# A transformer layer on one core: 52 unread products in two places, a lead-in four steps earlier, and stores issued past two barriers

## What is computed

```python
def layer(x, W_attn, b_attn, W_proj, b_proj, fast_b, w_fc, w_proj, u, v, gate):
    x = x + attention(layernorm(x))          # 16 heads of 16, causal, float32 softmax, then @ W_proj + b_proj
    h = layernorm(x)
    a = bitlinear(h, w_fc) + gate * (h @ v.T @ fast_b.T @ u.T)     # 256 -> 1024
    r = maximum(a, 0.0)
    return x + bitlinear(r * r, w_proj)      # 1024 -> 256
def bitlinear(x, w):   # rows of w become -s, 0 or s with s = mean |w| of the row
    s = clip(mean(abs(w), axis=1), 1e-5)
    return x @ (s * clip(round(w / s), -1, 1)).T
```

## Time and profile before

| | us |
|---|---|
| median of 3 runs | 2120.4 |
| lowest and highest | 2115.23 and 2132.78 |
| the profiled execution, its own time | 2129.81 |
| its span in the trace | 2128.1 |
| busy in the span: PE, DVE, ACT, POOL | 2032.3, 1850.8, 1487.4, 474.8 |
| mean granted clock of TensorE | 0.967 of full |

### The profile page before, as it was taken

One profiled execution on the slowest core, in us unless ns is written; L12 is line 12 of the kernel. 1 busy time (PEld: TensorE's weight loads), 2 busy tenths in 40 slices (PEclk: granted clock), 3 DMA queues, 4 the chain that ended last, 5 costly groups with the idle time before them and its releaser, 6 DMA issues. The chain is left out here.

```text
span 2128.1 us, 46470 instructions
## 1 busy us (share of the span) xinstructions
PE 2032.3 (96%) x18173; PEld 1123.1 (53%) x18173; DVE 1850.8 (87%) x3143; ACT 1487.4 (70%) x2787; POOL 474.8 (22%) x637
## 2 busy tenths in 40 slices
PE   6987899999999999999999999999999969999998
PEld 5875344444444444444444444444444438888887
DVE  7987889999999999999999999999999438998996
ACT  2331378888888888888888888888888535555554
POOL 0000011011110111111011110111111127776774
PEclk9997599999999999999999999999999779999999
DMA  5995121221222212122121211212122122333220
GB/s 192 325 317 215 29 54 47 53 57 38 75 52 60 55 40 65 48 70 47 53 60 34 82 51 54 57 37 71 50 63 62 36 65 80 101 89 90 80 80 30
DMA packets 163003, 168.29 MB, mean 79 GB/s; under 512 B 74704, under 2 KB 102880, under 8 KB 162784
## 3 DMA queue, kind: packets, MB, share of 16 engines
q1 hardware_dynamic: 154112, 157.72, 25.4%
q10 hardware_dynamic: 8672, 7.60, 1.3%
HBM read 95.77 MB, written 67.63 MB: 77 GB/s over the span
## 5 line engine op out<-in xcount | busy, mean ns | idle before, releaser
L984 ACT ACTIVATE probs<-ps_s 128x512 f32<-128x512 f32 x2176 | 1179.3, 596 | 257.8 <-PE ps_s L1177 231.8
L1010 DVE TENSOR_REDUCE maxes<-ps_m 128x2 f32<-128x1024 f32 (+1 forms) x960 | 1141.9, 1220 | 110.5 <-PE ps_m L1140 88.4
L1198 PE MATMUL ps_acc<-probs,vs 128*32 128x256 f32 (+1 forms) x8696 | 703.9, 396 | 11.9 <-ACT acc_sb L962 11.9
L1177 PE MATMUL ps_s<-qs,ks 50*128 50x512 f32 (+3 forms) x2560 | 577.8, 450 | 1.0 <-ACT probs L984 0.9
L1140 PE MATMUL ps_m<-ks,qs 48*128 48x512 f32 (+3 forms) x2560 | 504.4, 392 | 18.7 <-DVE maxes L1010 9.5
L1177 PEld LDWEIGHTS ps_s<-qs,ks 50*128 50x128 f32 x2560 | 255.9, 186 | 414.0 <-ACT probs L984 381.1
L1198 PEld LDWEIGHTS ps_acc<-probs,vs 128*32 128x32 f32 x8696 | 173.7, 108 | 295.1 <-issue 194.7
L918 POOL TENSOR_SCALAR_AFFINE_SELECT probs<-probs 128x512 f32<-128x512 f32 x256 | 160.0, 640 | 744.1 <-ACT probs L984 740.5
L1140 PEld LDWEIGHTS ps_m<-ks,qs 48*128 48x128 f32 x2560 | 265.1, 192 | 94.5 <-DVE maxes L1010 70.7
L1017 DVE CUSTOM_DVE_ANT_0 sums_masked<-ps_m,mask 128x384 f32<-128x384 f32 (+1 forms) x512 | 186.6, 421 | 20.2 <-PE ps_m L1140 4.1
L1382 POOL TENSOR_TENSOR hid<-square,hid 128x512 fp32r<-128x512 f32 x128 | 175.3, 1378 | 107.3 <-DVE square L1393 91.9
(11 more groups left out here) (129 smaller groups left out, 1764.5 us busy)
## 6 DMA issues: line engine op xcount, KB each, us to landing
qs<-q_scr SPq DMA_DIRECT2D x384, 64.0 KB, 2.7
...
```

Source lines behind the costliest of these rows:

```text
L984: act.activation(probs[:, s % RING, x], ps_s[:, k % BANKS], ACT.Exp).then_inc(ring_taken, 1)
L1010: last = dve.tensor_reduce(maxes[c % 2][:, :, pairs, tt, i], banks, AX.X, ALU.max)
L1177: last = pe.matmul(ps_s[:, k % BANKS, at:at + width], ks[u][rows, j // TT, p, j % TT * P:(j % TT + 1) * P], qs[u][rows, c, p, q0:q0 + widt ...
L1198: last = pe.matmul(ps_acc[h * VW:(h + 1) * VW, q0:q0 + width], vs[u][:, j, h], probs[:, s % RING, h % banks_of(s), at:at + width], start=( ...
```

## The change

The new function `fill` issues products of 128 x 128 weights by 512 columns of `w_o` into a bank of PSUM that nobody reads before it is written anew. They wait for nothing and signal nothing. Three of them follow each of the last ten items of the opening (30 in all), two stand at each place for values of the first three steps of unit 0 (10), and two follow steps 17, 18, 19, 32, 33 and 34 of the last unit (12).

The places of the last unit move: turning u from step 17 to 16, its product from 22 to 20, w1 from 25 to 21, w2 from 29 to 25, the scales from 33 to 29, the projection from 34 to 31, and with them the loads and copies of chunk 0 (o from step 19 to 20, x from 22 to 24). DVE takes the factor (`take_low_factor`) before the second ternary weight. DVE's part of the projection, residual and variance is at step 31 and no longer behind the last step. The load and scaling of chunk 1's attention result go into the last unit (SP at step 32, POOL after its last step). ACT takes the root ahead of the last copy of the accumulator. At the start of feed-forward ACT copies `xn_t` ahead of chunk 1's o.

SP's stores of chunk 15 go to the start of block 2, and those of the last accumulator and reciprocal to the start of block 3, the reciprocal itself too (DVE). In block 1 the twelve small DMAs go from ACT to SP, ahead of SP's first store; PE's transposes of chunk 1 go behind chunk 0's products of q and k; and DVE's scaling of the weights no longer waits for the load of `w_o`.

```diff
-LOADS_AT, TERNARY_AT, O_AT, X_AT = 5, 16, 19, 22
-LOW_AT, G_AT, W1_AT, W2_AT, S_AT, PROJECT_AT = 17, 22, 25, 29, 33, 34
-SCALE_AT, BIAS_AT, O_HIGH_AT = 26, 30, 33
+LOADS_AT, TERNARY_AT, O_AT, X_AT, O1_AT = 5, 16, 20, 24, 32
+LOW_AT, G_AT, W1_AT, W2_AT, S_AT, PROJECT_AT = 16, 20, 21, 25, 29, 31
+SCALE_AT, BIAS_AT, O_HIGH_AT = 25, 29, 29
+
+
+FILLED_ITEMS, FILLED_STEPS = 10, (17, 18, 19, 32, 33, 34)
...
+def fill(pe, w_o, bank, count):
+
+    for _ in range(count):
+        pe.matmul(bank, w_o[:, 0, 0, 0:P], w_o[:, 0].rearrange("p k d -> p (k d)"), start=True, stop=True, skip_group_check=True)
...
+def store_acc(sp, scr, lead, n, c):
+
+    sp.wait_ge(lead.acc_copied, NCH * n + c + 1)
+    acc_sb, sums = lead.acc_sb[c % 2], lead.sums[c % 2]
+    for h in range(GH):
+        sp.dma_start(sums[h * VW:(h + 1) * VW, :],
+                     acc_sb[h * VW + HD:h * VW + HD + 1, :].rearrange("o (x e) -> o x e", x=VW)).then_inc(lead.sums_in[c % 2], 16)
+    dst = scr["o"].rearrange("b g r (c s) -> b g c r s", s=CH)[bass.ts(n // GROUPS, 1), bass.ts(n % GROUPS, 1), c]
+    sp.dma_start(dst.rearrange("o i r s -> (o i r) s"), acc_sb[:]).then_inc(lead.acc_stored[c % 2], 16)
+
+
...
+def store_chunk(sp, scr, sh, n):
+
+    u = n % 2
+    for m in range(4):
+        sp.wait_ge(sh.l_done, 4 * n + m + 1)
+        dst = (scr["q"] if m < KD else scr["k"]).rearrange("b a (f d) (c s) -> b f c d a s", f=KD, s=CH)
+        dst = dst[bass.ts(n // NCH, 1), m % KD, bass.ts(n % NCH, 1)].rearrange("o i d a s -> (o i d) a s")
+        sp.dma_start(dst, sh.parts[u][:, m].bitcast(F32)).then_inc(sh.parts_stored[u], 16)
+    sp.wait_ge(sh.v_copied, 2 * n + 2)
+    dst = scr["v"].rearrange("b p (c t) d -> b c p t d", c=NCH)[n // NCH, n % NCH]
+    sp.dma_start(dst, sh.v_out[u]).then_inc(sh.v_stored[u], 16)
...
+            sp.dma_start(w_o_in[:], io["W_proj"].rearrange("(k p) n -> p k n", p=P)).then_inc(w_o_loaded, 16)
+
+            sp.wait_ge(masked, 3)
+            for r in range(2):
+                for half in range(2):
+                    for dst, src in ((sh.ident_half, keep["ident_h"]), (sh.mask_half, keep["mask_h"])):
+                        sp.dma_start(dst[ROW * r:ROW * (r + 1), half], src[ROW * half:ROW * (half + 1), :]).then_inc(sh.fixed_in, 16)
+            sp.wait_ge(sh.ones_set, 1)
+            load_ones(sp, sh, sh.ks)
...
+                if left > 0:
+                    store_chunk(sp, scr, sh, n)
...
-            dve.wait_ge(w_in, 16 * 2)
+            dve.wait_ge(w_qkv_loaded, 16)
...
-            act.wait_ge(masked, 3)
-            for r in range(2):
-                for half in range(2):
-                    for dst, src in ((sh.ident_half, keep["ident_h"]), (sh.mask_half, keep["mask_h"])):
-                        act.dma_start(dst[ROW * r:ROW * (r + 1), half], src[ROW * half:ROW * (half + 1), :]).then_inc(sh.fixed_in, 16)
-            act.wait_ge(sh.ones_set, 1)
-            load_ones(act, sh, sh.ks)
...
-                if left >= 1:
+                if left >= 1 and n > 0:
...
+                if n == 0:
+                    transposes(1, 1)
...
+            store_chunk(sp, scr, sh, BATCH * NCH - 1)
...
-                if last:
-                    store_acc(n, NCH - 1)
-                    store_recip(n, NCH - 1)
+                    if last and s == O1_AT:
+                        sp.wait_ge(late.w2_ready, KH // 2)
+                        load_o(sp, scr, lead.o_in[1], lead.r_in[1], lead.o_loaded[1], 1)
...
+                if last:
+                    scale_o(pool, lead.o_in[1], lead.r_in[1], lead.o_loaded[1], lead.o_scaled, 1)
...
                 if last:
+                    lead.norm.take_root(act, 0)
                     copy_acc(n, NCH - 1)
-                    lead.norm.take_root(act, 0)
...
+                        take_low_factor()
...
+                    if last and s == PROJECT_AT:
+                        copy_low(dve, lead.o_t, lead.o_in[0], lead.o_copied, lead.o_split, 0)
+                        for i in range(2):
+                            residual(dve, lead, lead.x, lead.x1, 0, i)
+                        lead.norm.variance(dve, 0)
                 if last:
-                    copy_low(dve, lead.o_t, lead.o_in, lead.o_copied, lead.o_split, 0)
-                    for i in range(2):
-                        residual(dve, lead, lead.x, lead.x1, 0, i)
-                    lead.norm.variance(dve, 0)
                     lead.norm.normalise(dve, lead.x1, lead.xn, 0).then_inc(lead.xn_ready, 1)
-                    invert(n, NCH - 1)
...
+                    if x[1] >= LEAD - FILLED_ITEMS:
+                        fill(pe, keep["w_o"], ps_acc[:], 3)
...
+                        elif what == "values":
+                            fill(pe, keep["w_o"], ps_acc[:], 2)
+                    if last and s in FILLED_STEPS:
+                        fill(pe, keep["w_o"], ps_m[:, 3], 2)
...
-            load(1)
+            load_x(sp, io, x[1], x_loaded[1], 1)
+            store_acc(sp, scr, lead, UNITS - 1, NCH - 1)
             for n in range(CHUNKS):
                 if n + 2 < CHUNKS:
 
                     sp.wait_ge(x1_ready, 2 * (n + 1))
                     load(n + 2)
+                if n == 0:
+                    store_recip(sp, scr, lead, UNITS - 1, NCH - 1)
...
-            scale(1)
...
+            invert_sums(dve, lead, UNITS - 1, NCH - 1)
...
-            act.wait_ge(o_ready, 2)
-            copy_high(act, o_t, o_in[1], o_scaled, o_copied, KD)
             for n in range(CHUNKS):
                 copy_high(act, xn_t, ps_t, turned, turned_copied, KD * n)
+                if n == 0:
+                    act.wait_ge(o_ready, 2)
+                    copy_high(act, o_t, o_in[1], o_scaled, o_copied, KD)
```

89 lines of the change are left out of this document (39 added, 50 removed).

## The result

| | before | after |
|---|---|---|
| median, us (20 executions each) | 2127.75 | 2109.91 |
| lowest and highest | 2112.72 and 2139.42 | 2103.06 and 2121.82 |
| the profiled execution, its own time | 2129.81 | 2109.09 |
| its mean granted clock | 0.967 | 0.981 |

The ratio is 0.9925, with a 95% interval of 0.9903 to 0.9946: the change is worth 11 to 21 us. I had forecast 2087 with a range of 2070 to 2109. The time lies just above the range. Between the two profiled executions 20.7 us went, where my sum had 38.3.

A forecast was written before the change was run, and what follows sets the result against it. PE was busy 99% in the steady units and, at 1.2 GHz, the bound in two half-clock stretches. Six terms took 38.3 us off 2129.8, giving 2091.5; the median forecast was 2087 us, range 2070 to 2109.

The forecast's parts named there:

- Opening and unit 0: Opening items and first unit: extra products restore full clock, 12.0 us gained, 2.0 charged; -10.0 us.
- ten items, 5.8 us: Upper end of the opening's cost: all ten filled items run at half clock, 5.8 us.
- The guess of 3.5 items: Opening: 3.5 filled items at half clock before the clock rises, charged 2.0 us.
- products don't raise the clock before 274 us: Rival, opening and unit 0: clock stays at half, gives back 12.0 us and costs 3.8 + 4.3 more; 2107 us, chance 0.10.
- Last unit: Last unit: w1 work moved earlier keeps full clock, its twelve products charged 1.5 us; -9.4 us.
- Start of block 1: Start of block 1: chunk 1's root no longer waits behind twelve DMA issues on ACT; -2.5 us.
- The barrier: First barrier, ahead of the opening: without chunk 15's five stores in front, DVE ends last; -3.5 us.
- The end of the unit: End of the last unit: root taken ahead of the last copy, transposes at full pace; -3.4 us.
- Feed-forward's start: Start of feed-forward: PE begins 13.7 us sooner, but waits for POOL's low parts; -9.5 us.
- single gap of 4 to 7 us on PE: Sign, feed-forward chunk 0: PE waits 4 to 7 us ahead of `second_layer`, released by POOL.

The follow-up runs named there:

- e7: Changed kernel with POOL's scaling of chunk 1's input behind the barrier into feed-forward instead of ahead of it; median 2108.75 us, ratio 0.9923.
- e4: Changed kernel with POOL's scaling of chunk 2 behind four of chunk 0's low parts instead of ahead of all eight; median 2103.49 us, ratio 0.9920.
- c1: The kernel before, unchanged, profiled a second time; one execution, 2121.42 us.
- p1: Kernel before with only unread products added: two beside all 40 opening items, four at each of five unit 0 places; 2150.34 us, ratio 1.0122.
- e3: Changed kernel without its twelve products in the last unit; median 2103.66 us, ratio 0.9894.
- b1: Changed kernel with two products beside all 40 opening items, four per unit 0 place, none in the last unit, both chunk scalings later, chunk 1's transposes earlier; 2086.92 us.
- b2: As b1, but three products per unit 0 place, and chunk 1's scaling and transposes placed as in the changed kernel; 2108.56 us, ratio 0.9834.
- f1: b1 with three products beside the first twelve opening items and two beside the other 28; median 2086.66 us, ratio 0.9852.
- f2: f1 with six more unread products at the end of block 1; median 2087.02 us, ratio 0.9852.
- e9: Changed kernel with chunk 1's transposes in block 1 behind twelve of chunk 0's products instead of 24; median 2101.41 us, ratio 0.9888.
- c2: The kernel before, unchanged, profiled a third time; one execution, 2123.64 us.

## Why the prediction was wrong, step by step

**Opening and unit 0: the step that failed.** It had three parts. Unit 0's gain was 10.9 us (B 42.0 to 31.1), forecast 12.0: right. The price per filled item failed. I wrote that PE needs 0.43 us of an item in columns and 1.71 with three products. But the earlier trace rows show an item busy for 0.79 of 1.13 us (0.73 by the pitch in the profile after), and three products between two items take 1.57 and not 1.29. That is 2.30, 1.17 over DVE's pace and not 0.58. And the clock rose after eight filled items, not 3.5. 8 x 1.17 = 9.4 us stand where I had 2.0. My own upper end, "ten items, 5.8 us", used the same wrong price. The guess of 3.5 items came from one row of feed-forward, where nothing but 128-row products ran. The six kernels with this opening show how little such a row binds: A is 54.5, 57.7, 58.5, 58.6, 59.5 and 62.1, that is three to ten filled items at half clock, and in e7 the clock was at 0.50 until 278 us. What decides when it rises stays open. I had a rival for that ("products don't raise the clock before 274 us", 0.10), priced it at 2107, and it was the nearest to the truth in time. In mechanism it is what happened in e7's profiled execution, not in the changed kernel's.

**Unit 0 can lose the clock again.** No case of mine had that. Of the changed kernel's 20 executions 13 took 2103.1 to 2113.2 us (mean clock 0.979 to 0.984) and seven 2117.8 to 2121.8 (0.973 to 0.977). Two profiles show ways to the second kind: in e4 the clock rose in time and fell again, 0.98 in the microsecond from 246 and 0.50 from 247 to 281 us; in e7 it did not rise before 278 us (2123.3 us, mean clock 0.974). Which of the two the seven took is not known. In B it costs 12 to 14 us (43.4 and 45.0 for 31.1), and it puts the median 3 us above the middle of the first kind, 2106.7.

**Last unit: the mechanism was right, its base was chance.** Forecast -9.4, in the pair of profiles -6.4. But c1 and p1 show the unit of before at 69.8 us when the clock stays, less than the changed kernel's 73.1. What the change brings there is only the absence of a fall that came in two of four executions, and it pays 3.9 us for twelve products in each. Against the mean of the four, 74.5, it is worth 1.4 us. The order alone seems to hold the clock: without products it stayed up in five profiles of five (e3, b1, b2, f1, f2), and at two in four that would be a chance of 3%. When it stays up anyway the order brings 0.6 us (69.8 to 69.2). I charged 1.5 us for the products on the ground that ACT and DVE leave PE slack; PE had no idle time in the stretch, which the same rows said.

**Start of block 1.** Forecast -2.5; the first bias copy of chunk 0 moved by 0.6 us, from 27.5 to 27.0 (26.3 to 28.3 in the ten profiles with this order), and the end of the block by nothing that its scatter of 4 us lets one see. I had written that the transposes now stand behind 24 products and costed it at part of the gain; it was nearly all of it. 1.5 us of it comes back in e9 and 2.5 to 3.1 us in b1, f1 and f2.

**Right steps.** The barrier (-3.7 for -3.5). The end of the unit but for 1.0 us: the root in front took 2.6 us off, and POOL's scaling of chunk 1, which the change put beside DVE's chain, gave 1.1 back; I had named the added scaling and not what it shares with DVE. Feed-forward's start (-8.7 for -9.5): POOL waited for `r_in` 8.4 us after its issue, 8.6 forecast from the earlier trace rows. The Trainium skill, "DMA: Bandwidth & Descriptors", section on the anatomy of one DMA, gives its 2.0 us plus bytes by bandwidth for DMAs that GpSimd issues, and these are SP's; my estimate of 4.4 us from it would have put the gain at 13.7. The wait looks otherwise than I said: no single gap of 4 to 7 us on PE, but four of 0.4 to 0.5 us, ahead of its work on the last four low parts. The steady units did not change.

**The base.** The sum was made against one execution of 2129.8 us in which the last unit had fallen. I took 4.5 us off the sum's 2091.5, because that execution lay 9.4 us above the median of three. The median of twenty is 2127.75, 2.1 us under it, so there was no ground for taking anything off; but even 2091.5 is 18 us under the measured time, and the ledger shows where they are: 8.6 in the opening and unit 0, 3.3 at the start of block 1, 3.0 in the last unit, 1.3 at its end, 0.8 in feed-forward, and the rest in stretches that scatter. The part of the sum that undoes chance falls should have been weighed by how often they come; one profile can't say, c1 and c2 could.
